# Two-layer transformer kernel: input loaded ahead of the weights, and 37 of 128 FFN-table entries unpacked outside the pass over the expert tiles

## The reference, cut to what matters

```python
# layer 0, attention: projections, causal convolution over 4 taps, rotations, a scan over the tokens
q, k = conv(x @ Wq), conv(x @ Wk);  v = conv(x @ Wv);  alpha, beta = sigmoid(x @ Wa), sigmoid(x @ Wb)
state = rotate(state, phi_t) * alpha_t + beta_t * rotate(v_t, psi_t);  out_t = rotate(state, -theta_t)
y = (out * rsqrt(mean(out**2)) * rms_w * silu(x @ Wg)) @ Wo
# layer 0, FFN: a router picks 2 of 16 experts for each token, 2 shared experts are added at 0.1
routed += mask[..., e] * (silu(x @ wg[e]) * (x @ wu[e])) @ wd[e]
# layer 1, attention: 16 heads, causal softmax
# layer 1, FFN: weights come as 4-bit indices into a table of 16 values
w = lut[idx];  out = (silu(x @ lut[gate_idx].T) * (x @ lut[up_idx].T)) @ lut[down_idx].T
```

## Time and profile before

| | us |
|---|---|
| median of 3 runs | 2424.4 |
| lowest and highest | 2420.91 to 2424.61 |
| the profiled execution, its own time | 2417.39 |
| its span, first to last instruction | 2415.6 |

### The profile page before, as it was taken

One profiled execution on the slowest core, in us unless ns is written; L12 is line 12 of the kernel. 1 busy time (PEld: TensorE's weight loads), 2 busy tenths in 40 slices (PEclk: granted clock), 3 DMA queues, 4 the chain that ended last, 5 costly groups with the idle time before them and its releaser, 6 DMA issues. The chain is left out here.

```text
span 2415.6 us, 36801 instructions
## 1 busy us (share of the span) xinstructions
PE 2184.5 (90%) x12802; PEld 1884.9 (78%) x12802; DVE 1891.7 (78%) x4233; ACT 1346.6 (56%) x3105; POOL 545.3 (23%) x516
## 2 busy tenths in 40 slices
PE   4789898588987999999999999999999999999996
PEld 3676666356656888889889888988988988898984
DVE  4888887747986888887887888788788788878763
ACT  3543434114554666775675576567567657756752
POOL 0211322410103323222321321222231132222110
PEclk9898998688998999999999999999999999999998
DMA  7001000226541112111111211111121121111100
GB/s 272 0 1 38 33 31 23 99 90 182 175 125 42 57 40 66 49 36 66 58 41 52 62 53 40 61 59 40 45 79 36 36 79 45 48 50 36 49 14 9
DMA packets 88532, 145.88 MB, mean 60 GB/s; under 512 B 8352, under 2 KB 55840, under 8 KB 88352
## 3 DMA queue, kind: packets, MB, share of 16 engines
q1 hardware_dynamic: 67104, 112.07, 14.5%
q0 software_dynamic: 6144, 16.79, 2.0%
q10 hardware_dynamic: 15104, 14.68, 1.8%
HBM read 105.76 MB, written 37.75 MB: 59 GB/s over the span
## 5 line engine op out<-in xcount | busy, mean ns | idle before, releaser
L850 ACT ACTIVATE pr<-bank,negmax 128x128 f32<-128x128 f32 (+3 forms) x512 | 265.9, 526 | 264.4 <-DVE negmax L1318 249.3
L541 POOL TENSOR_TENSOR wo_low<-wraw_o,wo_high 128x256 fp32r<-128x256 f32 x128 | 94.8, 740 | 927.9 <-ACT wo_high L586 927.9
L1318 DVE TENSOR_REDUCE negmax<-bank 128x1 f32<-128x128 f32 (+3 forms) x512 | 239.6, 489 | 13.1
L531 POOL TENSOR_TENSOR wqk_low<-wraw,wqk_high 128x512 fp32r<-128x512 f32 x128 | 165.6, 1294 | 338.5 <-ACT wqk_high L586 338.5
L966 DVE TENSOR_TENSOR p_low<-bank,p_high 128x512 fp32r<-128x512 f32 (+1 forms) x384 | 206.8, 593 | 9.1 <-ACT p_high L586 0.6
L1344 DVE SCALAR_TENSOR_TENSOR xs<-bank,rinv,xs 128x256 f32<-128x256 f32 x512 | 211.2, 475 | 1.2 <-PE bank L1461 1.2
L1459 PE MATMUL bank<-h_high,wqk_high 128*128 128x512 f32 x512 | 204.7, 400 | 2.2 <-DVE h_low L966 2.2
L1460 PE MATMUL bank<-h_low,wqk_high 128*128 128x512 f32 x512 | 204.1, 399 | 0.0
L1461 PE MATMUL bank<-h_high,wqk_low 128*128 128x512 f32 x512 | 203.7, 398 | 0.0
L1459 PE MATMUL bank<-wo_high,z_high 128*128 128x256 f32 x512 | 151.4, 296 | 50.4 <-issue 37.8
L586 ACT ACTIVATE p_high<-bank 128x512 fp32r<-128x512 f32 (+1 forms) x384 | 173.0, 529 | 0.7 <-PE bank L1752 0.7
(11 more groups left out here) (282 smaller groups left out, 6542.1 us busy)
## 6 DMA issues: line engine op xcount, KB each, us to landing
wraw<-in_wpair SPq DMA_DIRECT2D x64, 512.0 KB, 4.1
wraw<-in_wpair SPq DMA_DIRECT2D x64, 256.0 KB, 4.3
wraw_o<-in_wpair SPq DMA_DIRECT2D x64, 256.0 KB, 2.5
tokens_by_expert<-zero SPq DMA_DIRECT2D x10, 1024.0 KB, 10.7
xt<-tokens_by_expert SPq DMA_DIRECT2D x40, 256.0 KB, 3.2
expert_results<-ey ACTq DMA_DIRECT2D x40, 256.0 KB, 3.6
wres<-in_wexp SPq DMA_DIRECT2D x1, 6144.0 KB, 19.7
xs<-x_between_stages SPq DMA_DIRECT2D x8, 512.0 KB, 4.5
```

The lines of the kernel that those rows point to most:

```text
L531: pool.tensor_tensor(low, wraw[r][:, 2 * e * D:2 * (e + 1) * D], high.bitcast(F32), ALU.subtract).then_inc(s_wq, 1)
L541: pool.tensor_tensor(wo2[e][1][:], wraw_o[r][:, e, :], wo2[e][0][:].bitcast(F32), ALU.subtract).then_inc(s_wo, 1)
L850: ins = sc.activation(pr[:, i, 0:(i + 1) * P], score(i), ACT.Exp, bias=negmax[:, i:i + 1], accum_out=rsum[:, i:i + 1])
L1318: ins = v.tensor_reduce(negmax[:, i:i + 1], score(i), AX_X, ALU.max, negate=True)
```

## The change

Three things are done.

The first is the start. Unit 0 is loaded first. The constants are split: 4 that the first products need (`s_const`), then 11 others (`s_const2`). DVE runs `first_norm(0)` before any weight work; ACT applies the norm before it makes the high part of the weights. Scaling of the output weights goes behind `input_low(0)`. The clearing DMAs wait for `input_low(0)` (`s_hl` at 4) too.

The second is the table. 32 entries stand in five groups of 3, 8, 4, 9 and 8 among DVE's work on the last unit and behind it, and 5 stand behind the last tile. The pass keeps 91 entries for 80 tiles. The indices of chunks 0 and 1 are loaded during the last unit, after waits on PE's product counts; the other six loads are moved in SP's list.

The third is what makes this possible in memory: `w8`, `ge0` and `go0` stand where `fws` comes to lie, `fidx_bf` has 2 buffers instead of 8, and two fillers keep early writes off live tiles. SP's wait for the stored units (`s_x1s`) moves from ahead of the first tile to tile pair 10.

```diff
+EARLY_CHUNKS = 2
+EARLY_ENTRIES = (3, 8, 4, 9, 8)
+LATE_ENTRIES = 5
+INDEX_LOADS = (0, 1, 7, 13, 20, 27)
...
-        CONST_DMAS = 15
+        CONST_DMAS, CONST2_DMAS = 4, 11
...
+            load_unit(0)
+            for dst, src in ((w8raw[:, :, 0:6, :], w0), (wabs[:], wab), (cws[:], cw), (invfs[:], invf)):
+                sp.dma_start(dst, src).then_inc(s_const, 16)
...
-            sp.wait_ge(s_setup, 2)
+            sp.wait_ge(s_setup, 1)
+            sp.wait_ge(s_hl, 4)
...
                 if u == NU - 2:
+                    sp.wait_ge(s_pv, 12 * NU)
+                    sp.wait_ge(s_pg, 12 * NU)
+                    for c in range(EARLY_CHUNKS):
+                        load_indices(c)
                     sp.wait_ge(s_gm, RT * NU)
...
+            unit_apply(0, 0, xu[0], xn1, s_xn1, s_ln1)
             sc.wait_ge(s_setup, 2)
             high(w8[0][:].rearrange("p k q n -> p (k q n)"), w8raw[:].rearrange("p k q n -> p (k q n)"), s_w8h)
-            unit_apply(0, 0, xu[0], xn1, s_xn1, s_ln1)
...
+            def unpack_to(total):
+                for n in range(unpacked[0], total):
+                    c, e = divmod(n, LUTN)
+                    if e == 0:
+                        unpack_index(c)
+                    unpack_equal(c, e)
+                    unpack_add(c, e)
+                unpacked[0] = max(total, unpacked[0])
...
                 rotate_scan(x, r)
+            unpack_to(sum(EARLY_ENTRIES[:1]))
             rms(x)
             for r in range(RT):
                 gated(x, r)
             for ab in range(2):
+                unpack_to(sum(EARLY_ENTRIES[:ab + 2]))
                 residual(x, ab)
                 unit_stats(1, xu[x % 3], ab)
             unit_norm(1, s_ln2)
+            unpack_to(sum(EARLY_ENTRIES[:4]))
             router_picks(x)
...
+            early = sum(EARLY_ENTRIES)
+            unpack_to(early)
             for t in range(NTILE):
                 tile_product(t)
+                unpack_to(early + (t + 1) * (NB * LUTN - LATE_ENTRIES - early) // NTILE)
+            unpack_to(NB * LUTN)
```

More of the change, by code:

```diff
@@ L122, in two_layer_program @@
                 w8raw = raw.enter_context(nc.sbuf_tensor("w8raw", [P, KD, 8, ROW], F32))
-            ge, go = ([sa(f"{name}{i}", [P, RT, T]) for i in range(2)] for name in ("ge", "go"))
+            ge_even, go_even = (sa(name, [P, RT, T]) for name in ("ge0", "go0"))
+            w8 = [sa(f"w8_{part}", [P, KD, 8, ROW], F32R) for part in ("high", "low")]
+            ge_odd, go_odd = (sa(name, [P, RT, T]) for name in ("ge1", "go1"))
+            ge, go = [ge_even, ge_odd], [go_even, go_odd]
             ve, vo, sn, cs, al, be = (sa(name, [P, RT, T]) for name in ("ve", "vo", "sn", "cs", "al", "be"))
@@ L189, in two_layer_program @@
             ehT = [sx(f"ehT{i}", [P, P]) for i in range(2)]
+            sx("over_odd_gates", [P, 7 * P])
+            wres = sx("wres", [P, NEXP, EW])
+            sx("over_scratch", [P, 10 * T])
+            equal = [sx(f"equal{i}", [P, LC], BF16) for i in range(2)]
+            fidx_bf = [sx(f"fidx_bf{i}", [P, LC], BF16) for i in range(2)]
+            fidxs = sx("fidxs", [P, NB, LC], I32)
         def split(name, shape):
@@ L443, in _ @@
                              ).then_inc(s_xt[n % 4], 16)
-                if n == 1 or n % 5 == 0 and n // 5 < NB - 1:
-                    load_indices(n // 5 + 1 if n else 0)
+                if n == 10:
+                    for i in range(3):
+                        sp.wait_ge(s_x1s[i], 32 * len(range(i, NU, 3)))
+                if n in INDEX_LOADS:
+                    load_indices(EARLY_CHUNKS + INDEX_LOADS.index(n))
                 if n in (24, 28):
@@ L929, in _ @@
             v.memset(all_bf[:], 1.0).then_inc(s_setup, 1)
[L930 to L938, removed]
-            v.tensor_scalar(cws[:, :, 0], cws[:, :, 0], invfs[:, 0:1], -1.0, ALU.mult, ALU.mult)
-            v.tensor_scalar(cws[:, :, 1], cws[:, :, 1], invfs[:, 0:1], None, ALU.mult).then_inc(s_setup, 1)
-            v.wait_ge(s_setup, 2)
-            v.wait_ge(s_w8h, 1)
-            v.tensor_tensor(w8[1][:], w8raw[:], w8[0][:].bitcast(F32), ALU.subtract).then_inc(s_w8l, 1)
             linked = [0]
@@ new lines, in unpack_add @@
+            def unpack_add(c, e):
+                n = c * LUTN + e
+                dst = fws[:, c * LC:(c + 1) * LC]
+                v.wait_ge(s_leq, n + 1)
+                if e == 0:
+                    v.tensor_scalar(dst, equal[n % 2][:], luts[:, e:e + 1], None, ALU.mult).then_inc(s_lut, 1)
+                else:
+                    v.wait_ge(s_lut, n)
+                    v.scalar_tensor_tensor(dst, equal[n % 2][:], luts[:, e:e + 1], dst, ALU.mult, ALU.add
+                                           ).then_inc(s_lut, 1)
@@ new lines, in _ @@
+            v.tensor_scalar(cws[:, :, 0], cws[:, :, 0], invfs[:, 0:1], -1.0, ALU.mult, ALU.mult)
+            v.tensor_scalar(cws[:, :, 1], cws[:, :, 1], invfs[:, 0:1], None, ALU.mult).then_inc(s_setup, 1)
+            v.wait_ge(s_setup, 2)
+            v.wait_ge(s_w8h, 1)
+            v.tensor_tensor(w8[1][:], w8raw[:], w8[0][:].bitcast(F32), ALU.subtract).then_inc(s_w8l, 1)
+            input_low(0)
+            v.wait_ge(s_const2, 16 * CONST2_DMAS)
+            v.tensor_copy(before[:], before32[:])
@@ L1160, in _ @@
+            for par in range(2):
+                v.tensor_scalar(wo_all[:, par, :], wo_all[:, par, :], rmsws[:, par:par + 1], None, ALU.mult)
+                v.tensor_scalar(wo_rest[:, par, :], wo_rest[:, par, :], rmsws[:, par:par + 1], None, ALU.mult)
             for r in range(RT):
```

79 lines of the change are left out of this document (31 added, 48 removed).

## The result

| | changed kernel | kernel before |
|---|---|---|
| median of its runs | 2402.99 us (2401.53 to 2406.29) | 2422.65 us (2419.06 to 2424.61) |
| ratio | 0.9928, 95% interval 0.9917 to 0.9940 | 1 |
| profiled execution | 2404.1 us, span 2402.4 | 2417.4 us, span 2415.6 |

The ratio, applied to the 2424.4 us against which the prediction was made, gives 2406.9: 17.5 us less (14.5 to 20.1), where the prediction had 31.3 and a range that ended at 2405. The direction was right and the size was not. (The two medians of the table are 19.7 us apart, the two profiled executions 13.3; the ratio lies between.)

A forecast was written before the change was run, and what follows sets the result against it. DVE was taken to bound the pass at 1.92 us per tile, and one serial chain the start. -9.8 + 0.3 + 0.5 - 20.9 - 1.7 + 0.3 = -31.3 us; 2424.4 - 31.3 = 2393, range 2386 to 2405.

The forecast's parts named there:

- The start: Start of layer 0: with unit 0 loaded first, the first product comes at 26.5 instead of 36.35, 9.8 us less.
- The slower clock: Start of layer 0: PE may stay longer at 1.2 GHz after its longer idle stretch, 0 to 1 us, taken as 0.
- The last unit: Last unit of layer 0: five early groups hidden in DVE's idle time, costing only +0.3 (group 1) and +0.5 (group 5).
- my second rival: Last unit and tail: DVE and POOL lock each other out, scatters taking 1.96 each; 5.7 us more, 2399; chance 0.12.
- The pass: Tiles 5 to 79: with 91 entries PE becomes the bound at 1.63 us a step, 126.6 against 147.5, 20.9 less.
- the three steps around tile 40: Pass, around t = 40: the event's loss of 5.5 us stays, so three steps take 10.4 us instead of 11.25.
- the 0.5 for the casts: Pass: three casts of 0.45 us fall on double tiles and add 0.5 us in sum.
- The first rival: Pass does not reach PE's pace, ACT's four operations and a store must fit; 1.80 a step, 12.1 more, 2405; chance 0.14.
- Wrong if steps average over 1.75: Pass: sign that would refute the prediction, which expected tiles to open 1.63 us apart in long runs.
- the last unit grows by more than 2 us: Last unit: sign that would refute the prediction, which expected about 79 us from last scan to expert_row, unchanged.
- The slower rival: Last unit: indices land late and early entries block DVE's list; slower than before, for instance 2430; chance 0.01.
- The tail: Behind tile 79: last store after about 5.5 us, 1.7 less; late entries beside the first gathers add 0.3.

The follow-up runs named there:

- e1: The changed kernel run once more, with nothing altered, for a second time and trace: 2398.51 us, ratio 0.9930 to the kernel before.
- e2: The changed kernel with all 128 table entries left in the pass, so the new start alone: ratio 0.9963 to the kernel before.
- e3: The changed kernel with its start put back as it was, so the moved table entries alone: ratio 0.9961 to the kernel before.
- e6: The changed kernel, read kept, with all table entries of the pass but each chunk's first cut to one column: ratio 0.9908 to the kernel before.
- e7: The changed kernel with the read of a tile's expert moved to the end of the step, behind the down product: ratio 0.9884 to the kernel before.
- e4: The changed kernel without the read of each tile's expert, a number of the program instead: 2381.38 us, ratio 0.9862 to the kernel before.
- e8: The changed kernel with six experts packed per word, 14 reads ahead of the first tile, shift and mask in the pass: ratio 0.9871 to the kernel before.
- e5: The kernel before without the read of each tile's expert, a number of the program instead: ratio 1.0002 to the kernel before.
- e11: The changed kernel with every tile's expert read twice in a row at the same place: ratio 1.0066 to the kernel before.
- e9: e8 with two words read ahead of the first tile and one more at the end of every sixth step: ratio 0.9861 to the kernel before.

## Why the prediction failed, by its steps

Of all traces, e1 stands best beside the trace of before, because neither has the held addition. From trace to trace, in us:

| term | predicted | e1 | first trace after |
|---|---|---|---|
| first product | -9.8 | -10.0 | -10.2 |
| from there to the first tile | +0.8 | +1.7 | +4.1 |
| first five tiles | 0 | -0.5 | -0.2 |
| tile 5 to tile 79 | -20.9 | -8.7 | -8.0 |
| tile 79 to last store | -1.7 | -1.5 | -1.5 |
| last store to first mix | +0.3 | +0.2 | +0.2 |
| from first mix to the end | 0 | -0.1 | +2.4 |
| sum | -31.3 | -18.9 | -13.2 |

**The start** was right, each link within 0.3 us of its estimate. The slower clock, bounded at 0 to 1 us and taken as 0, did cost a little behind the first product: the products took 0.63 us each at first and 0.39 later, and the change came 3.6 us after the first product before, 4.0 in the first trace after and 4.8 in e1. By the thirteenth product after the first that was 0.2 and 0.6 us.

**The last unit** was right in mechanism. At `slots` the lead on the kernel before (527.10) was 9.8 us in the first trace (517.34) and 8.3 us in e1 (518.81). Most of that difference stood before group 1: at the end of the last scan the leads were 9.9 and 8.7 us. The rest is the mutual lock, met in e1 and missed in the first trace. VectorE (first) and GpSimd (second) in e1's group 1:

```profile
459.28 2.75 DVE L1170 TENSOR_SCALAR equal<-fidx_bf 128x576 bf16<-128x576 bf16 x1
...
462.80 0.20 DVE L1057 TENSOR_SCALAR va<-bank 128x48 f32<-128x48 f32 x1
```

```profile
459.36 1.28 POOL L509 TENSOR_TENSOR ge<-ge,oe 128x512 f32<-128x512 f32 x1
460.59 1.26 POOL L509 TENSOR_TENSOR go<-go,oo 128x512 f32<-128x512 f32 x1
```

A compare of 0.30 us took 2.75, until GpSimd's two products were over, and `va` came 5.95 us behind the end of the scan instead of 4.85 (first trace, e2 and before). By `slots` only 0.3 us of it was left. The Trainium skill ("SBUF — State Buffer", "Who interferes with whom") states that a VectorE instruction in a 2-port mode and a GpSimd instruction hold each other off for the whole instruction; e1 agrees for this compare beside GpSimd's `tensor_tensor`. Four of the ten traces that have group 1 met it (e1, e3, e6, e7). The scatters do not show the 1.96 us that my second rival took from the earlier trace rows: beside group 5 the last two took 1.10 and 0.99 us in e1, and 1.20 at most in e3. That rival was not the cause.

**The pass** is the step that failed: "Steps: 71 x 1.63 = 115.7". The 1.63 was real, and e4 and e8 run at it. It was not a pace of the kernel with the read. In the trace of before such a step (under 1.66 us) was followed by one of 2 us or more in 17 of 22 cases, and I had explained every slow one by VectorE's second entry. "PE's matmuls are back to back in such a step" was true of the fast step alone, and the sequencer's read of the expert stood in my sum at nothing, without a reason. In its place the runs show a read that, with its check, holds the turn back in nearly every second step: 138.8 - 124.0 = 14.8 us, by the view of waits 14.2 us (e1, 29 times). The miss of 12.2 us comes out of e1 like this: the 71 steps took 131.0 us instead of 115.7, 15.3 more; the three steps around tile 40 took 7.8 instead of 10.4, 2.6 less; and the 0.5 for the casts does not show.

**The first rival** had the size: its pass is 8.8 us shorter and its sum -19.2, beside 8.7 and -18.9 in e1. In part that is luck, since outside tile 40 the steps took 1.85 on average and not 1.80 (3.2 us more), which the dearer event in the sum (2.6 us) and the casts made up for. Its mechanism was another: not ScalarE's four operations, which fit into 1.63 (e4, e8), but the sequencer's read. My range ended at this rival's 2405 and left no room for anything beside it, such as the +1.7 (e1) or +4.1 us up to the first tile; the result, 2406.9, lies 2 us above. "Wrong if steps average over 1.75" was the sign that showed it. The sign "the last unit grows by more than 2 us" came up too, in the first trace alone: from the last scan to `expert_row` 87.1 us instead of 79.1, through the held addition (79.5 in e1).

**The slower rival** did not occur: the early groups stood in their places, with no wait for indices ahead of them.

**The tail** was right: 5.67 us from tile 79 to the last store against 5.5 predicted, and 7.3 to the first mix against 7.1 (7.4 by the +0.3 in the sum).

**Open** is the held addition. It is in the profiled executions of the changed kernel's first run and of e5 to e11, and not in those of the kernel before and of e1 to e4. e5 has the table and the start of the kernel before, so it is no effect of the change. e1 to e4 ran on one chip, e5 to e8 on a second and e9 to e11 on a third, so it may go with the chip or the moment. In all of them the addition starts 2.6 to 2.8 us behind the end of the last scatter's issue, with TensorE's product for it long done. In e5 (VectorE's row, then GpSimd's last scatter):

```profile
548.02 1.29 DVE L1155 SCALAR_TENSOR_TENSOR xs<-bank,xs 128x512 f32<-128x512 f32 x2 [9.35 <-remote]
```

```profile
544.26 0.96 POOL L510 DMA_INDIRECT tokens_by_expert<-xm,slots  x1 [0.30 <-issue]
```

The traces don't name what holds it, and no run here took the scatters away from it. Against e1 it cost the first trace some 2 us at the first tile. The 2.4 us between first mix and end in that trace I can't explain either; the kernels differ by up to 5 us in layer 1, which the change does not touch (1661.8 in e3 to 1666.9 in e2 from the first `negmax` on).

## What to carry to other kernels

A fast step taken from a trace is a floor, not a pace: look at what follows it, and put the mean over pairs of steps into the sum, above all where something is done once for two tiles. When an edit frees one engine, list what the next engine's sequencer does in a step, register reads among it, and not only its busy time; idle time "for issue" at one line, even 3.7 us of it, is the sign. In this kernel the values that the control sequence needs were best read in bulk where the engine waits anyway and unpacked in registers (e8).

## What was not expected of the hardware

- A read of one word from memory by TensorE's sequencer lasts 0.30 us in most cases and about 1.0 us where it begins 1.0 to 1.3 us behind the issue of a tile pair's load and a store (29 of 29 long reads in e1); with nothing queued on TensorE it lasted 0.71 and 0.90 us right behind a load (e8). Four products queued ahead of it are not enough to lengthen it (41 reads of 0.30 us in e1). A second read and its check in each step cost 0.43 us a step (e11); shift and mask cost nothing visible (e8).
- Two limits 6% apart (147 and 139 us for the same stretch) hide each other: without the read alone the time is the same (1.0002, e5), the entries alone give 0.4% (e3), and both together 1.0% beyond the start (0.9862 in e4, 0.9963 in e2).
- A 0.30 us compare was held 2.75 us beside two GpSimd products, in one execution (e1) and not in another of the same program.
- The lead that a shorter start gave changed by up to 2.6 us through layer 0 (12.6 and 10.0 at `va` of units 1 and 2), as TensorE's stretches with a granted clock of 0.50 fell in other places.
